# All regular transposes of a macaron block moved from TensorE to VectorE squares and SBUF transfers

## What is computed

```python
x = x + 0.5 * ffn(_layernorm(x))
x = x + mixer(_layernorm(x))
x = x + 0.5 * ffn(_layernorm(x))
```

```python
gate, val = split(x @ W_in.T)
v = depthwise_conv(val, 5 taps) + conv_b
h = tanh(a_param) * h + sigmoid(gate) * v      # a scan over the tokens
res = x + y @ W_out.T                          # y: all h
mixer(x) = layernorm(res) * ln_w + ln_b
```

## Time and profile before

| | us |
|---|---|
| median of 3 executions (lowest, highest) | 674.28 (674.20, 674.43) |
| the profiled execution | 674.34 |
| its span in the trace | 672.5 |
| TensorE busy in it | 656.8 (98%) |
| VectorE, ScalarE, GpSimd busy | 550.6, 419.4, 444.9 |

### The profile page before, as it was taken

The page is one execution under the profiler, slowest core; times in us unless marked ns, Lnnn a source line. Parts: engine busy times, 40 slices in busy tenths (PEclk is TensorE's granted clock), DMA queues, the critical chain, the costliest instruction groups (busy, mean ns, idle before and its releaser), DMA issues. The chain is left out here.

```text
span 672.5 us, 9867 instructions
## 1 busy us (share of the span) xinstructions
PE 656.8 (98%) x3048; PEld 530.6 (79%) x3048; DVE 550.6 (82%) x1545; ACT 419.4 (62%) x800; POOL 444.9 (66%) x444
## 2 busy tenths in 40 slices
PE   7899999999999999999999999999999999999997
PEld 6687888888888887888888888888878778777785
DVE  5888889988978888889779798688989967967765
ACT  3656576675576656766567765767576576655554
POOL 1256558775676776766767766868676777676654
PEclk9899999999999999999999999999999999999999
DMA  8100100100001000010001000000000000100001
GB/s 215 53 17 20 32 0 21 33 20 17 4 18 32 20 17 21 1 44 9 16 21 31 21 1 24 13 17 20 17 9 13 1 20 3 34 1 17 20 1 31
DMA packets 24853, 15.55 MB, mean 23 GB/s; under 512 B 6592, under 2 KB 21856, under 8 KB 24800
## 3 DMA queue, kind: packets, MB, share of 16 engines
q1 hardware_dynamic: 24224, 14.90, 7.7%
q10 hardware_dynamic: 576, 0.02, 0.1%
HBM read 11.83 MB, written 3.08 MB: 22 GB/s over the span
## 5 line engine op out<-in xcount | busy, mean ns | idle before, releaser
L564 POOL TENSOR_TENSOR hid_lo<-hid,hid_hi 128x512 fp32r<-128x512 f32 x270 | 348.6, 1295 | 192.3 <-ACT hid_hi L671 191.9
L820 DVE TENSOR_TENSOR weighted<-gate_ps,wb 128x512 f32<-128x512 f32 x256 | 175.1, 684 | 68.6 <-ACT gate_ps L663 63.6
L663 ACT ACTIVATE gate_ps<-gate_ps 128x512 f32<-128x512 f32 x256 | 148.7, 581 | 122.4 <-PE gate_ps L1109 119.3
L671 ACT ACTIVATE hid_hi<-hid 128x512 fp32r<-128x512 f32 x272 | 170.5, 627 | 61.0 <-DVE hid L833 56.6
L833 DVE TENSOR_TENSOR hid<-weighted,up_ps 128x512 f32<-128x512 f32 x256 | 174.4, 681 | 8.4 <-POOL hid_lo L564 0.5
L1177 PE MATMUL down_ps<-hid_lo,wt_hi 128*128 128x512 f32 x272 | 107.9, 397 | 0.2 <-DVE hid_lo L841 0.2
L1174 PE MATMUL down_ps<-hid_hi,wt_hi 128*128 128x512 f32 x272 | 107.7, 396 | 0.0
L1175 PE MATMUL down_ps<-hid_hi,wt_lo 128*128 128x512 f32 x272 | 107.5, 395 | 0.0
L1107 PE MATMUL gate_ps<-xT_hi,wt_hi 128*128 128x512 f32 x170 | 71.9, 423 | 0.0
L1107 PE MATMUL up_ps<-xT_hi,wt_hi 128*128 128x512 f32 x170 | 68.4, 402 | 2.3 <-DVE hid L833 2.3
L1108 PE MATMUL gate_ps<-xT_lo,wt_hi 128*128 128x512 f32 x170 | 67.4, 397 | 0.0
(11 more groups left out here) (194 smaller groups left out, 1104.0 us busy)
## 6 DMA issues: line engine op xcount, KB each, us to landing
wb<-wT_hbm SPq DMA_DIRECT2D x60, 64.0 KB, 2.1
x_ln<-in_L_attn_x SPq DMA_DIRECT2D x8, 256.0 KB, 3.1
x_res<-in_L_attn_x SPq DMA_DIRECT2D x8, 256.0 KB, 2.8
out_x<-x SPq DMA_DIRECT2D x7, 256.0 KB, 2.3
raw_gate<-in_L_ffn_gate_w SPq DMA_DIRECT2D x4, 256.0 KB, 4.7
raw_up<-in_L_ffn_up_w SPq DMA_DIRECT2D x4, 256.0 KB, 5.0
raw_down<-in_L_ffn_down_w SPq DMA_DIRECT2D x4, 256.0 KB, 5.2
wT_hbm<-wT SPq DMA_DIRECT2D x15, 64.0 KB, 1.5
```

What stands on the lines that cost most here:

```text
L564: nc.gpsimd.tensor_tensor(hid_lo[s][:, :], hid[s][:, :], hid_hi[s][:, :].bitcast(F32), ALU.subtract)\
L663: nc.scalar.activation(bank[:, :] if j else silu_sb[:, :], bank[:, :], ACT.Silu).then_inc(silu_done, 1)
L671: nc.scalar.activation(hid_hi[s][:, :], hid[s][:, :], ACT.Copy).then_inc(hid_hi_done, 1)
L820: V.tensor_tensor(weighted[j % 2][:, :], gate_ps[n % BANKS][:, :], wb[u % 2][:, :], ALU.mult)\
```

## The change

A block's tokens are now dealt to partitions in another order (token = 4 x partition + t), so that a load of x is one contiguous 2 KB run per partition. A 128x512 transpose is then made in two parts: VectorE transposes all 32x32 squares in one instruction (`shuffle_*`), and SP moves the squares between the four groups of 32 partitions by 16 DMAs of 32x128 (`move_*`). The tables name the first "shuffle", and SP follows their slots.

- Moved are the normed input of 6, 5 and 4 blocks (k = 1, 2, 4), the first FFN's output of 6, the second's of 7, the mixer's output of 4 (`MOVED_*`). The others stay on TensorE.
- The router of 12 blocks and the mixer's output of 4 hold the weights stationary: three 128x512 matmuls. The router's weights are loaded four times, and ScalarE copies 32x128 pieces of the result (`spread_logits`), which VectorE then transposes (`shuffle_logits`).
- The routing weights of all 15 later units are transposed by VectorE (`shuffle_weights`) and spread by 16 DMAs from SBUF, without the way over HBM.
- The low part of a moved input (`xT_low_moved`) and the sums with moved outputs (`first_ffn_sum`, `mixer_sum`, `output_add`) are GpSimd's; `halve_ffn` and `wT_copy` are gone from ScalarE.
- Slots that matter: in (4,b) units shuffle ffn 1 at 3.5 (its sum at 7), shuffle 2 at 7 (xT high 2 at 10), shuffle 4 at 14 (xT high 4 at 0 of the next unit), weights 1 at 14.5; in (1,b) units shuffle ffn 4 at 4, shuffle mixer at 9.5 (sum at 12), store at 10, shuffle 1 at 11 (xT high 1 at 0 of the next unit), weights 4 at 15. In `BEGIN` weights 1 stands at 14 and shuffle 1 at 14.5 (first unit) or 15.5 (second); in the fourth, weights 4 at 15 and shuffle 1 at 15.5. The weights are used from tile 1 of the next unit on.

```diff
+MOVE = QUADS * QUADS * 16
+MOVED_NORM = {1: range(2, NBLK), 2: range(1, NBLK - 2), 4: range(1, 5)}
+MOVED_FFN = range(1, NBLK - 1)
+MOVED_MIX = range(1, 5)
+SPREAD = {1: range(2, NBLK), 4: range(1, NBLK - 1)}
...
-    x_blk = x.rearrange("a s d -> (a s) d").rearrange("(n t p) d -> n p t d", t=TT, p=P)
+    x_blk = x.rearrange("a s d -> (a s) d").rearrange("(n p t) d -> n p t d", t=TT, p=P)
...
+        PREPARE = {"xT high 1": 0, "low 1": 0, "router 1": 2, "spread logits 1": 2, "shuffle logits 1": 3,
+                   "silu logits 1": 5, "route 1": even(4, 14), "weights 1": 14.5}
...
+            def move_norm(k, b):
+                n = b - MOVED_NORM[k][0]
+                sp.wait_ge(x_shuffled[k], n + 1)
+                sp.wait_ge(xT_lo_done[k], b)
+                for src in range(QUADS):
+                    for dst in range(QUADS):
+                        sp.dma_start(moved_x[k][QUAD * dst:QUAD * dst + QUAD, P * src:P * src + P],
+                                     shuffled_x[k][QUAD * src:QUAD * src + QUAD, P * dst:P * dst + P])\
+                          .then_inc(x_moved[k], 16)
...
             def broadcast_weights(k, b):
                 u = ORDER.index((k, b))
-                sp.wait_ge(wT_done[k], b + 1 if k == 4 else b)
-                if u > 1:
-                    sp.wait_ge(wb_loaded[(u - 1) % 2], u // 2 * 64)
-                sp.dma_start(wT_hbm.rearrange("e (t p) -> (e t) p", t=TT), wT[k][:, :]).then_inc(wT_stored, 16)
-                sp.wait_ge(wT_stored, u * 16)
+                sp.wait_ge(w_shuffled[k], b + 1 if k == 4 else b)
                 if u > 1:
                     sp.wait_ge(weighted_done, (u - 1) * NPAIR)
-                for n in range(SPLIT):
-                    sp.dma_start(wb[u % 2][n:P:SPLIT, :], wT_hbm).then_inc(wb_loaded[u % 2], 16)
+                for src in range(QUADS):
+                    for n in range(SPLIT):
+                        sp.dma_start(wb[u % 2][n:P:SPLIT, P * src:P * src + P],
+                                     wS[k][QUAD * src:QUAD * src + QUAD, :]).then_inc(wb_loaded[u % 2], 16)
...
+            def xT_low_moved(k, b):
+                pool.wait_ge(xT_hi_done[k], b + 1)
+                nc.gpsimd.tensor_tensor(lo_of(k, b), moved_x[k], hi_of(k, b).bitcast(F32), ALU.subtract)\
+                  .then_inc(xT_lo_done[k], 1)
...
             def xT_high(k, b):
+                if b in MOVED_NORM[k]:
+                    act.wait_ge(x_moved[k], (b - MOVED_NORM[k][0] + 1) * MOVE)
+                    if k == 2:
+                        act.wait_ge(mix_val_ready, b)
+                    elif unread(k, b):
+                        act.wait_ge(up_ready, unread(k, b) * NT)
+                    nc.scalar.activation(hi_of(k, b), moved_x[k], ACT.Copy).then_inc(xT_hi_done[k], 1)
...
+            def shuffle_norm(k, b):
+                n = b - MOVED_NORM[k][0]
+                dve.wait_ge(ln_normed[k], b + 1)
+                if n > 0:
+                    dve.wait_ge(x_moved[k], n * MOVE)
+                V.transpose(shuffled_x[k].rearrange("p (b r t) -> p t b r", b=QUADS, t=TT),
+                            by_dim(normed[k][:, :, :])).then_inc(x_shuffled[k], 1)
...
+                if b in SPREAD[k]:
+                    product(side[:, :], wt_hi[:, WROUTER, :], hi_of(k, b), lo_of(k, b), wt_lo[:, WROUTER, :],
+                            True, True).then_inc(logits_made[k], 1)
+                    return
```

More of the change, by code:

```diff
@@ L335, in macaron_kernel @@
[L335 to L341, removed]
@@ new lines, in macaron_kernel @@
+        PREPARE = {"xT high 1": 0, "low 1": 0, "router 1": 2, "spread logits 1": 2, "shuffle logits 1": 3,
+                   "silu logits 1": 5, "route 1": even(4, 14), "weights 1": 14.5}
+        BEGIN_NEXT = {"stats 1": 15, "meanvar 1": 16}
+        MIXER = {"conv": (0, 0.5, 1, 2, 3, 4.5), "y high": 6, "y low": 6, "mixer out": 8, "shuffle mixer": 9.5,
+                 "sum mixer": 12, "stats 3": 13, "meanvar 3": 14.5, "norm 3": 15}
+        ROUTE4 = {"xT high 4": 0, "low 4": 0, "router 4": 2, "spread logits 4": 3, "shuffle logits 4": 3.5,
+                  "silu logits 4": 5, "route 4": even(4.5, 14.5), "weights 4": 15}
@@ L355, in macaron_kernel @@
                 ({"conv": (15, 15.5, 16.5, 16.5, None, None)}, 0),
[L356 to L358 removed]
+                ({"xT high 1": 0, "low 1": 0, "router 1": 2, "spread logits 1": 2, "shuffle logits 1": 3,
+                  "silu logits 1": 4, "route 1": even(3, 13), "weights 1": 14}, 2),
+                ({"stats 1": 11, "meanvar 1": 12.5, "norm 1": 12, "normalise 1": 14, "next x_ln": 15.5,
+                  "shuffle 1": 15.5}, 3),
             ],
@@ L445, in macaron_kernel, with xn_count @@
         LOGITS_READ = 2
+        def xn_count(k, b):
+            return sum(i not in MOVED_NORM[k] for i in range(b + 1))
         MIX = K + 1
@@ L589, in unit @@
                 for j in range(NT):
+                    for n in (1, 2, 4):
+                        for b in due(steps, f"low {n}", j):
+                            xT_low_moved(n, b)
+                    for b in due(steps, "sum ffn 1", j):
+                        first_ffn_sum(b)
+                    for b in due(steps, "sum mixer", j):
+                        mixer_sum(b)
                     for b in due(steps, "norm 3", j):
@@ L1010, in beside @@
                     dve.wait_ge(x_res_loaded, b * 16 + 16)
-                    dve.wait_ge(ffn_transposed[1], b + 1)
+                    dve.wait_ge(ffn_transposed[1], sum(i not in MOVED_FFN for i in range(b + 1)))
                     if b >= 2:
@@ L1028, in beside @@
                         recur(b, mixing)
+                for n in (1, 4):
+                    for b in due(steps, f"weights {n}", slot):
+                        shuffle_weights(n, b)
                 for k in LN:
```

347 lines of the change are left out of this document (227 added, 120 removed), and 3 rows, old and new, of the table END.

## The result

| | us |
|---|---|
| before, median of 4 (lowest, highest) | 674.24 (672.88, 674.43) |
| after, median of 4 (lowest, highest) | 904.14 (903.01, 908.13) |
| ratio, 95% interval | 1.342 (1.340 to 1.345) |
| the profiled execution after, its span | 904.98, 903.2 |

The change makes the kernel 230 us slower. The direction was forecast, the size was not: 735 was said, and 904 lies above the range too.

The account below looks back on a forecast made before the run. TensorE was taken as the bound, busy 656.8 of 672.5 us. From 674.34 us, 25.8 removed and 86.9 added gave 735 us; forecast 718 to 769 (chance 0.5), 8-in-10 range 664 to 800.

Parts of the forecast that it names:

- What TensorE gives back: On TensorE: removed transposes 12.0 us, router and mixer matmuls 10.2, weights transposes 3.6; 25.8 us saved in sum.
- The sum of 25.8: Total us taken from TensorE by removed transposes (12.0), fewer router and mixer matmuls (10.2) and weights transposes (3.6).
- the idle 18% hides: On VectorE: 12.8 us more work on 550.6 was to fit in its idle time without becoming the bound.
- Stalls, start and clock: SP-queue stalls, three more loads at the start (1.4 us) and TensorE's lowered clock (17.0): 86.9 us added in all.
- (a) to (c): SP-queue stalls: moved input behind weights at the start 25.5 us, weights behind a moved input 24.6, three in a row 14.9.
- (c): Units (1,4) to (1,6): weights 4 queue behind mixer's move, store and shuffle 1; 4.95 us lost three times, 14.9.
- The cover: Lateness that doesn't reach TensorE: 2.2 us when VectorE waits for weights, 2.6 when ScalarE waits for a moved input.
- The pitch: On the SP queue: time from one 32x128 DMA issue to the next, taken as 0.47 us.
- Rival 3: SP trains cost as wb's loads do, pitch 0.63 us with landing at 2.1: 830 us; chance 0.12.
- Rival 1: All moves on the SP queue are covered, as at a pitch of 0.22 us: 650 us, faster; chance 0.2.

Follow-up runs that it names:

- e2: Changed kernel with one transfer per move and per spread of routing weights instead of sixteen, exchange of squares between partition groups left out: 709.69 us.
- e14: e2 with TensorE's stationary columns read side by side instead of every fourth, leaving out the new token order there: 698.78 us.
- e13: e2 with the third unit's steps after the first FFN's move put 1 to 2.5 slots earlier: 701.50 us.
- e7: e2 with VectorE's transposes cut from 128x512 to 128x128: 703.15 us.
- e11: e2 with the turned router logits put in PSUM instead of SBUF: 703.63 us.
- e15: e2 with the four edits of e14, e11, e13 and e7 together: 673.97 us.
- e5: Changed kernel with 12 of the 16 transfers of each train, squares that stay in their own quadrant left out: 811.35 us.
- e1: Changed kernel with four transfers per move instead of sixteen, same bytes, exchange of squares between partition groups left out: 712.55 us.

## Why the prediction was wrong

By its own steps, 735.4 before rounding = 648.5 without the queue + 86.9 for the queue:

1. **What TensorE gives back, with engines that hide the rest** (forecast 648.5, e2 709.7: 61.2 us short). Two steps failed here. In e2 TensorE is busy 10.0 us more than before, where 25.8 less was forecast, and idle 25.4 us more, where nothing was: 35.8 + 25.4 = 61.2. The sum of 25.8 put the stationary columns, which the new token order leaves four apart, at no cost: 96 loads of 0.12 us, 10.9 us of time (e14). And "the idle 18% hides" was wrong: I added up busy times and asked whether an engine becomes the bound; I should have asked of each step in which slot it stands and who waits there. Shown, one by one: 8.2 us for slots moved to leave room (e13); 6.5 for three quarters of the transposes' length (e7), taken at 0.69 and measured at 1.10; 6.1 for logits read beside GpSimd (e11). VectorE's busy time rose by 28.6 us, where 12.8 was said (12.7 by its own rows). About 25 of the 61.2 stay open (e15).
2. **Stalls, start and clock at the forecast's own trains** (86.9 against 101.7, e5 less e2). Items (a) to (c) named the right places: the input behind the weights at the start, the weights behind shuffle 4 and behind three trains. Their sizes were mixed, and the near match of the sums is in part luck: (c) was far too dear in e5, and waits taken as covered came in its place. The cover was mixed too. In the changed kernel VectorE's waits for weights of 9.4, 8.5 and 9.1 us in (4,1) to (4,3) became 6.0, 5.1 and 5.8 on TensorE, 3.3 us covered where I took 2.2. Of ScalarE's 106.1 us, 83.2 got through to TensorE's products of these inputs, 1.8 covered per wait where I took 2.6: in the program such a product waits for `xT_lo` itself, and no second bank stands between.
3. **The pitch** (0.47 taken, 0.63 measured: 92.8 us, sixteen against twelve transfers). This was the largest miss. I chose the row of the same shape and put the weights' loads, 0.59 and a gap of 0.04, at the upper end; that end was the value. Rival 3 had this pitch at 0.12 and said 830. Its queue, 181.5 us over 648.5, is near the 194.4 measured over e2; what it lacked was step 1.

648.5 + 61.2 + 101.7 + 92.8 = 904.2; the pieces are differences of single executions (e2, e5), so they add up by construction. Rival 1 (all covered, 650) could not have come true at any pitch: e2 issues one transfer per move and takes 709.7. Of what was to be seen, ScalarE's waits came in the second, third and fifth unit, with 14.6 to 18.8 us instead of some 10. TensorE's idle time (65 or more up) was 179 up and its busy time 52 up instead of 26 down; of these 52, 42 are gone in e2, where the clock is at 0.99.

The Trainium skill's sentence on initiation (DMA: Bandwidth & Descriptors, section Issuing engines are not separate DMA queues), which the prediction weighed, holds for a lone transfer here (0.6 us against 1.8) and not for sixteen. Its advice to coalesce (the same page, Rules for kernel authors) is what e1 did: the same bytes in a quarter of the transfers, 192 us less, though without the exchange of squares.

One sum would have warned of it. A pair of units sends eight trains: 8 x 16 x 0.63 = 81 us of SP alone, where a pair took 79.3 us before (and takes 113 after). At 0.47 it is 60, and I had not added it up.

## What to carry to other kernels

Treat an issuing queue as an engine: count issues per period, take the pitch from a row with the same kind of source and destination, not the same shape, and ask at which pitch a period no longer fits. Before moving work to an engine that "has room", look at the slot it will stand in, at whether its operands are strided in SBUF, and at whether it will read SBUF beside GpSimd. A part of a rejected change can still pay: stationary router weights gained 0.5% in the eight blocks whose units got shorter with them, and lost in the four whose units got longer.

## What was not expected of the hardware

- The pitch of SP's issues goes with where a transfer comes from and where it goes, hardly with its size: 0.43 to 0.47 us for loads from HBM into neighbouring partitions, 0.63 into every fourth; from SBUF to SBUF 0.63 at 16 and 64 KB, 0.67 at 4 KB.
- float32 at a distance of 16 bytes in SBUF: VectorE's transpose 1.10 us instead of 0.71 (that one from PSUM), its `xT_lo` 1.10 instead of 0.69, ScalarE's copy out of PSUM 1.09 instead of 0.60, TensorE's weight load 0.33 instead of 0.19.
- VectorE's short operations on SBUF waited up to 1.1 us for GpSimd; from PSUM they took 0.25 to 0.29 us each time.
